# Moving two batches of normalisation statistics on VectorE to other steps of a scan pipeline

## Chip, cores and metric

The kernel runs on one NeuronCore of a Trainium2 chip. The metric is device time in microseconds (us) of one execution, 494.55 us for the kernel before. Five engines work side by side, each through its own queue in order: TensorE (PE in the profile), VectorE (DVE), ScalarE (ACT), GpSimd (POOL) and SyncE (SP), which here only issues DMAs. They meet by semaphores.

## The reference, cut to what matters

Two rows of 2048 tokens with 128 features go through an adaptive layer norm, a Mamba block (a selective scan with 256 inner channels and 16 states), a second adaptive layer norm and a soft decision tree of depth 8.

```python
h = _layernorm(x, axis=-1) * (1 + ca) + sa              # the first norm
xz = h @ W_in;  xp, z = jnp.split(xz, 2, axis=-1)
u = silu(causal_depthwise_conv(xp));  dt_r, Bm, Cm = split(u @ W_xp, ...)
delta = softplus(dt_r @ W_dt + dt_bias)
h_t = exp(delta * A) * h_(t-1) + delta * u * B_t;  y_t = sum_n(h_t * C_t)   # 16 states n, 256 channels
x = x + ga * ((y + u * D_skip) * silu(z)) @ W_out
h = _layernorm(x, axis=-1) * (1 + cb) + sb              # the second norm
gate = sigmoid((h @ Wq.T) @ routers.T);  leaf_prob = product of branch probabilities along each path
x = x + gb * (leaf_prob @ leaf_values @ Wout_w.T + Wout_b)
```

(The lines are shortened; `_layernorm` subtracts the mean over the 128 features and divides by the root of the variance plus 1e-5.)

## The kernel before

The 4096 tokens are cut into 8 groups of 512 (g = 0 to 7, four for each row of the batch). The scan of a group is 32 steps: step s handles state n = s // 2 and half s % 2 of the 256 channels, as a tile of 128 channels by 512 tokens. A main loop over g and s is written out for each engine, and what an engine does is decided by step numbers in tables. In step s of group g:

- ScalarE makes the decay `dA` = exp(delta * a) for the step two ahead (L697, `AHEAD_EXP` = 2) into one of three PSUM banks (`RD` = 3). It may write the bank of step s + 2 once the scan of step s - 1 is done.
- VectorE runs the scan `h` (L1382) with `dA` and `dbu`, and in even steps, for 11 of the 16 states, makes the product `dbu` (L1395) from a PSUM bank `bb` that TensorE has filled (L1148) with B.
- GpSimd makes `dbu` for the other five states (L593) and, when both halves of a state are scanned, the product `hc` = h * C (L606).
- TensorE adds `hc` up in `yb` (L1123), five steps behind the scan.

Beside the scan of group g each engine does its share of the front of group g + 1 (norm, convolution, silu, delta) and of the tail of group g - 1 (second norm, tree) and g - 2. Two of ScalarE's steps hold long blocks, because they change its function table and change it back: step 10 (`F_SILU`: a table load, silu of u and of z, a table load, L764 to L769) and step 17 (`F_SP`: a table load, the softplus of the next delta, from group 2 on also two softplus of the tree, a table load, L794 to L803). In step 10 the exp of scan 12 is issued ahead of the block and that of scan 13 behind it; in step 17 the exp of scan 19 ahead and that of scan 20 behind.

The norms' statistics are made by VectorE in `stats()`: four `bn_stats` (L1254) and four `bn_aggr` (L1257), on tiles of 128 tokens by 128 features. They stand at the end of a step, behind the scan and behind the `dbu` product of that step:

```python
if 4 <= g + 4 < GROUPS and s == N_STATS:          # first norm, of the group four ahead: in g = 0 to 3
    stats(g + 4, f_bn, f_mv[:, g + 4, :, :], s_fvar)
if tail and s == T_STATS:                         # second norm, of group g - 1: in g = 1 to 7
    wait_read(dve, "t", "out", 0, t)
    stats(t, t_bn, t_mv, s_tvar)
```

From the second norm's statistics ScalarE makes 1/sqrt in three small operations (`rstd`, L628 to L630, at `T_RSTD`; the third writes `t_nm`), GpSimd one small product (`t_offset`, L513, at `T_OFF`, ahead of the step's large products), and ScalarE normalises (`t_xhat`, L635, at `T_XHAT` = 24). GpSimd's queue waits at L513 until ScalarE's `rstd` is through. In the last group (g = 7) `rstd`, offset and normalisation stand at steps of their own, `LAST_RSTD`, `LAST_OFF` = 16 and `LAST_XHAT` = 17. The statistics of the first norm are used two groups later than they are made.

Of the kernel before, what the change touches and what calls it, by code (L numbers as in the profile page):

```python
# [7 lines left out]
def bass_adaln_mamba_tree_ffn_kernel(  # L8
# [72 lines left out]

    N_STATS, N_RSTD, N_OFF, N_XHAT = 19, 2, 3, 6
    F_SILU, F_SP, F_DU = 10, 17, (25, 26)
    F_HI, F_R1, F_MID, F_R2, F_LO = 21, 22, 23, 24, 25
    T_GATE, T_STATS, T_RSTD, T_OFF, T_XHAT = (4, 5), 14, 19, 20, 24
    NORMS = {2: (4, 3)}
    NORMS.update({g: (g + 1, g) for g in range(4, GROUPS)})

# [16 lines left out]
    FIRST, LAST = -1, GROUPS - 1  # L107
# [3 lines left out]
              ("node", 1, -1, (23,)), ("lp", 0, -1, (27,)), ("lp", 1, -1, (29,)), ("ff", 0, -1, (STEPS,)))  # L111
    LAST_SP = {2: -2, 25: -1}
    TOKENS = (slice(0, T // 2), slice(T // 2, T))
    LAST_RSTD, LAST_OFF, LAST_XHAT = 16, 16, 17

    def jobs_of(side, g):

# [24 lines left out]
    with ctx:  # L142
# [213 lines left out]
        def wait_job(eng, side, name, part, g):  # L356

            eng.wait_ge(s_job[side], job_at[side, name, part, g] + 1)

        def wait_read(eng, side, name, part, g):  # L360

            eng.wait_ge(s_read[side], read_at[side][job_at[side, name, part, g]])
# [13 lines left out]
        def saves(pair):  # L376

            g, n = divmod(pair, N)
            return (g // CHUNKS) * (CHUNKS - 1) * N + (g % CHUNKS) * N + (n if saved(pair) else 0)

        def saved(pair):

            return pair // N % CHUNKS < CHUNKS - 1

        def by_pool(pair):

            return pair // N * NB + sum(n < pair % N for n in POOL_N)

        def by_dve(pair):

            return pair - by_pool(pair)
# [846 lines left out]
        def _(dve):  # L1238
# [11 lines left out]
            def stats(g, bn, mv, ready):  # L1250
                if g:
                    dve.wait_ge(ready, g)
                for i in range(TILES):
                    last = v.bn_stats(bn[:, i, :], xs[:, g * TILES + i, :])  # L1254
                chain(last)
                for i in range(TILES):
                    last = v.bn_aggr(mv[:, i, :], bn[:, i, :])  # L1257
                last.then_inc(ready, 1)
# [100 lines left out]
            for g in range(FIRST, LAST + 1):  # L1359
                m2, f, t, u = g + 2, g + 1, g - 1, g - 2  # L1360
                norm, tail, leaf = 2 <= m2 < GROUPS, 0 <= t < GROUPS, 0 <= u < GROUPS
                for s in range(STEPS):
                    k = g * STEPS + s
                    if 0 <= k < K:
                        n, half = divmod(s, HALVES)
                        pair = k // HALVES
                        dve.wait_ge(s_dA, k + 1)
                        if half == 0:
                            if n in POOL_N:
                                dve.wait_ge(s_pdbu, by_pool(pair) + 1)  # L1370
                            else:
                                dve.wait_ge(s_dbu, by_dve(pair) + 1)
                            if pair >= RH:

                                dve.wait_ge(s_hc, pair - RH + 1)
                                if saved(pair - RH):
                                    dve.wait_ge(s_save, saves(pair - RH) + 1)
                            if g % CHUNKS:

                                dve.wait_ge(s_save, saves(pair - N) + 1)  # L1380
                        start = state[:, n, half:half + 1] if g % CHUNKS else 0.0
                        v.tensor_tensor_scan(h[:, pair % RH, half, :], dA[k % RD][:, :], dbu[:, pair % RW, half, :],  # L1382
                                             start, ALU.mult, ALU.add).then_inc(s_scan, 1)
                    kd = k + AHEAD_DBU
                    if 0 <= kd < K and kd % HALVES == 0 and kd // HALVES % N not in POOL_N:
                        pair = kd // HALVES
                        gd, n = divmod(pair, N)
                        if n == 0:
                            dve.wait_ge(s_du, HALVES * (gd + 1))
                        mine = by_dve(pair)  # L1390
                        dve.wait_ge(s_fill, mine + 1)
                        if pair >= RW:

                            dve.wait_ge(s_scan, HALVES * (pair - RW + 1))
                        v.tensor_tensor(dbu[:, pair % RW, :, :], du[:, gd % 2, :, :],  # L1395
                                        bb[mine % RB][:, :].unsqueeze(1).broadcast_to([P, HALVES, T]),
                                        ALU.mult).then_inc(s_dbu, 1)
                    if 4 <= g + 4 < GROUPS and s == N_STATS:
                        if g == 0:
                            dve.wait_ge(s_x, 16 * (GROUPS - 4))  # L1400
                        stats(g + 4, f_bn, f_mv[:, g + 4, :, :], s_fvar)
                    if tail and s in T_GATE:

                        half = T_GATE.index(s)
                        hg = HALVES * t + half
                        dve.wait_ge(s_sum, t * STEPS + STEPS - HALVES + half + 1)
                        dve.wait_ge(s_zsilu, t + 1)
                        if t:
                            wait_job(dve, "t", "yt", half, t - 1)
                        else:  # L1410
                            dve.wait_ge(s_wturn, 2)
                        v.tensor_tensor(yg[:, half, :], yb[hg % RY][:, :], zu[:, t % 2, half, :],
                                        ALU.mult).then_inc(s_gate, 1)
                    if tail and s == T_STATS:

                        wait_read(dve, "t", "out", 0, t)
                        stats(t, t_bn, t_mv, s_tvar)
# [69 lines left out]
```

## Time and profile before

| | before |
|---|---|
| median of 3 runs | 494.55 us (493.66 to 495.66) |
| the profiled execution, its own time | 495.33 us |
| its span in the trace | 493.5 us |
| mean granted TensorE clock | 0.941 of full speed |
| VectorE, ScalarE, GpSimd, TensorE busy | 91%, 77%, 86%, 82% |

The span is what the trace covers; the 1.8 us between it and the execution's own time lie around it. All positions below are us from the span's start. A row of a timeline gives start, length from the first start to the last end, engine, source line and operation, output<-inputs with sizes, and how many instructions were merged (x2); in square brackets stands how long the engine sat idle ahead of it and which instruction ended that wait.

### The profile page before, as it was taken

What the parts mean: (1) busy time and instruction counts of PE and PEld (TensorE: products, weight loads), DVE (VectorE), ACT (ScalarE), POOL (GpSimd) and SP (SyncE); (2) the same over time, 40 slices, a digit from 0 to 9 for tenths busy, and PEclk for the clock granted to TensorE, in tenths of its full rate; (3) what the DMA queues carried; (4) which work ended last, traced back from release to release, by engine and by line L of the source; (5) the groups of instructions that cost most, each with busy time, mean ns of one, the idle gap of its engine ahead of it and who ended that gap; (6) DMA issues with size and microseconds to landing.
All of it is one profiled execution on the core that took longest, in us unless ns stands there. A gap on an engine that the chain in (4) does not pass through costs nothing. (4 is left out here: it accounts for less than half of the span.)

```text
span 493.5 us, 6708 instructions
## 1 busy us (share of the span) xinstructions
PE 406.7 (82%) x2133; PEld 279.7 (57%) x2164; DVE 447.3 (91%) x539; ACT 378.1 (77%) x690; POOL 422.7 (86%) x236
## 2 busy tenths in 40 slices
PE   7969665997499698997799788996899697687796
PEld 3537444675358456674558556664658455565474
DVE  6698899979999899989999889988999889999852
ACT  4478975598867898698967898698966898687715
POOL 6159899999999789998999899988999789999810
PEclk9999987997889989998999999998999989599799
DMA  6673045200830028300742027300741027300001
GB/s 168 160 298 151 1 144 222 87 0 1 301 126 27 0 42 327 108 0 2 248 149 77 2 66 303 106 2 0 259 156 60 1 62 306 107 2 21 0 1 43
DMA packets 24146, 51.06 MB, mean 103 GB/s; under 512 B 4521, under 2 KB 14256, under 8 KB 20016
## 3 DMA queue, kind: packets, MB, share of 16 engines
q1 hardware_dynamic: 24112, 50.64, 30.1%
q8 instruction: 17, 0.28, 0.2%
q14 instruction: 17, 0.14, 0.1%
HBM read 48.01 MB, written 2.62 MB: 103 GB/s over the span
## 5 line engine op out<-in xcount | busy, mean ns | idle before, releaser
L606 POOL TENSOR_TENSOR hc<-h,c_rows 128x1024 f32<-128x1024 f32 x127 | 298.4, 2366 | 27.0 <-DVE h L1382 26.3
L1382 DVE TENSOR_TENSOR_SCAN h<-dA,state,dbu 128x512 f32<-128x512 f32 x192 | 234.2, 1266 | 13.2 <-ACT dA L697 13.2
L697 ACT ACTIVATE dA<-delta,a_neg 128x512 f32<-128x512 f32 x256 | 173.2, 685 | 45.3 <-DVE h L1382 44.9
L1123 PE MATMUL yb<-ident,hc 128*128 128x128 f32 x1024 | 155.1, 287 | 17.8 <-POOL hc L606 16.6
L1123 PEld LDWEIGHTS yb<-ident,hc 128*128 128x128 f32 x1024 | 131.0, 149 | 64.9 <-issue 45.0
L1395 DVE TENSOR_TENSOR dbu<-du,bb 128x1024 f32<-128x1024 f32 x88 | 105.5, 1199 | 3.7 <-PE bb L1148 2.0
L593 POOL TENSOR_TENSOR dbu<-du,b_rows 128x1024 f32<-128x1024 f32 x40 | 94.6, 2364 | 4.1 <-DMA b_rows<-bc_dram 4.1
L1382 DVE TENSOR_TENSOR_SCAN h<-dA,dbu 128x512 f32<-128x512 f32 x64 | 74.2, 1205 | 5.5 <-ACT dA L697 5.4
L1023 PE MATMUL mf<-f_hT,w_conv 128*128 128x512 f32 x112 | 54.6, 612 | 2.0 <-ACT zu L757 1.4
L1148 PE MATMUL bb<-b_parts,sel 128*128 128x512 bf16 x63 | 25.1, 399 | 37.7 <-DVE dbu L1395 36.4
L1148 PEld LDWEIGHTS bb<-b_parts,sel 128*128 128x128 bf16 x88 | 8.6, 98 | 56.5 <-DVE dbu L1395 36.9
L1023 PEld LDWEIGHTS mf<-f_hT,w_conv 128*128 128x128 f32 x112 | 19.7, 195 | 17.8 <-issue 14.5
L749 ACT ACTIVATE zu<-mf,cbias 128x512 f32<-128x512 f32 x14 | 9.5, 682 | 18.2 <-PE mf L1023 18.2
L999 PE MATMUL mt<-node_s,path 128*128 128x512 f32 x28 | 16.5, 674 | 7.4 <-ACT probT L833 5.0
L1040 PE MATMUL mf<-zu,w_xp 128*128 128x512 f32 x28 | 21.1, 846 | 1.0 <-ACT delta L794 1.0
L1034 PE MATMUL mf<-w_in,f_hT 128*128 128x128 f32 x128 | 17.7, 281 | 3.4 <-ACT zu L757 3.2
L1113 PEld LDWEIGHTS yb<-diag_d,zu 128*128 128x128 f32 x128 | 17.7, 208 | 3.2 <-issue 2.3
L1113 PE MATMUL yb<-diag_d,zu 128*128 128x128 f32 x128 | 18.9, 295 | 0.0
L703 ACT ACTIVATE state<-h 128x2 f32<-128x2 f32 x96 | 18.5, 193 | 0.2
L1034 PEld LDWEIGHTS mf<-w_in,f_hT 128*128 128x128 f32 x128 | 15.6, 191 | 5.2 <-ACT zu L757 5.2
L1074 PE MATMUL mt<-t_hT,w_node 128*128 128x512 f32 x28 | 15.9, 651 | 2.5 <-ACT node_x L840 2.0
L1048 PE MATMUL mt<-zu,w_xdt 128*128 128x512 f32 x28 | 15.0, 618 | 3.1 <-ACT xs L819 1.6
(206 smaller groups left out, 524.2 us busy)
## 6 DMA issues: line engine op xcount, KB each, us to landing
c_rows<-bc_dram SPq DMA_DIRECT2D x32, 1024.0 KB, 7.5
b_rows<-bc_dram SPq DMA_DIRECT2D x40, 256.0 KB, 8.9
xs<-in_L_attn_x_dram SPq DMA_DIRECT2D x8, 256.0 KB, 3.6
out_dram<-xs SPq DMA_DIRECT2D x7, 256.0 KB, 5.6
ygT<-in_L_attn_conv_w_dram SPq DMA_DIRECT2D x2, 256.0 KB, 4.3
bc_dram<-xd SPq DMA_DIRECT2D x8, 64.0 KB, 1.6
w_in<-in_L_attn_W_in_dram SPq DMA_DIRECT2D x2, 128.0 KB, 4.2
probT<-in_L_wmod_dram SPq DMA_DIRECT2D x1, 256.0 KB, 4.2
```

The costliest lines, as they stand in the source:

```text
L593: nc.gpsimd.tensor_tensor(dbu[:, pair % RW, :, :], du[:, gd % 2, :, :], b_rows[:, i, :].unsqueeze(1).broadcast_to([P, HALVES, T]), ALU.mul ...
L606: nc.gpsimd.tensor_tensor(hc[:, pair % RC, :, :], h[:, pair % RH, :, :], c_rows[:, q, n % NQ, :].unsqueeze(1).broadcast_to([P, HALVES, T]) ...
L697: nc.scalar.activation(dA[ke % RD][:, :], delta[:, ge % 2, half, :], ACT.Exp, scale=a_neg[:, half, n:n + 1]).then_inc(s_dA, 1)
L703: nc.scalar.activation(state[:, pair % N, :], h[:, pair % RH, :, T - 1], ACT.Copy).then_inc(s_save, 1)
L1023: last = nc.tensor.matmul(bank[:, :], w_conv[:, tap, part * P:(part + 1) * P], f_hT[:, tap:tap + T], start=tap == 0, stop=tap == TAPS - 1)
L1034: last = nc.tensor.matmul(bank[:, i * P:(i + 1) * P], f_hT[:, HALO + i * P:HALO + (i + 1) * P], w_in[:, DI + part * P:DI + (part + 1) * P] ...
L1040: last = nc.tensor.matmul(bank[:, :], w_xp[:, piece, :], zu[:, g % 2, HALVES + piece, :], start=piece == 0, stop=piece == HALVES - 1)
L1113: nc.tensor.matmul(bank[:, tile], zu[:, gs % 2, HALVES + half, tile], diag_d[:, half, :], start=tile.start == 0, stop=False, skip_group_ch ...
L1123: last = nc.tensor.matmul(bank[:, tile], hc[:, pair % RC, half, tile], ident[:, :], start=False, stop=n == N - 1, is_transpose=True, skip_ ...
L1148: nc.tensor.matmul(bb[mine % RB][:, :], sel[:, n, :], b_parts[:, gf % 2, :], start=True, stop=True).then_inc(s_fill, 1)
L1382: v.tensor_tensor_scan(h[:, pair % RH, half, :], dA[k % RD][:, :], dbu[:, pair % RW, half, :], start, ALU.mult, ALU.add).then_inc(s_scan, 1)
L1395: v.tensor_tensor(dbu[:, pair % RW, :, :], du[:, gd % 2, :, :], bb[mine % RB][:, :].unsqueeze(1).broadcast_to([P, HALVES, T]), ALU.mult).t ...
```

## The change

The first norm's statistics go from step 19 to step 12, the second norm's from step 14 to step 19, except in the last group, where they stay at 14 under the new name `LAST_STATS`. `rstd` of the second norm goes from step 19 to 21 on ScalarE and its offset from 20 to 22 on GpSimd; `T_XHAT` stays.

```diff
-    N_STATS, N_RSTD, N_OFF, N_XHAT = 19, 2, 3, 6
+    N_STATS, N_RSTD, N_OFF, N_XHAT = 12, 2, 3, 6
     F_SILU, F_SP, F_DU = 10, 17, (25, 26)
-    T_GATE, T_STATS, T_RSTD, T_OFF, T_XHAT = (4, 5), 14, 19, 20, 24
+    T_GATE, T_STATS, T_RSTD, T_OFF, T_XHAT = (4, 5), 19, 21, 22, 24
...
-    LAST_RSTD, LAST_OFF, LAST_XHAT = 16, 16, 17
+    LAST_STATS, LAST_RSTD, LAST_OFF, LAST_XHAT = 14, 16, 16, 17
...
-                    if tail and s == T_STATS:
+                    if tail and s == (LAST_STATS if g == LAST else T_STATS):
```

On VectorE, group 2, from the `dbu` product of step 12 to the scans behind step 19, the rows of before (the operation SCALAR_TENSOR_TENSOR on `h` is the scan):

```order
L1395 TENSOR_TENSOR dbu<-du,bb 128x1024
L1382 SCALAR_TENSOR_TENSOR h<-dA,state,dbu 128x512 x2
L1254 BN_STATS t_bn<-xs 128x6 x4
L1257 BN_AGGR t_mv<-t_bn 128x2 x4
L1382 SCALAR_TENSOR_TENSOR h<-dA,state,dbu 128x512 x2
L1395 TENSOR_TENSOR dbu<-du,bb 128x1024
L1382 SCALAR_TENSOR_TENSOR h<-dA,state,dbu 128x512 x2
L1395 TENSOR_TENSOR dbu<-du,bb 128x1024
L1382 SCALAR_TENSOR_TENSOR h<-dA,state,dbu 128x512
L1254 BN_STATS f_bn<-xs 128x6 x4
L1257 BN_AGGR f_mv<-f_bn 128x2 x4
L1382 SCALAR_TENSOR_TENSOR h<-dA,state,dbu 128x512 x3
```

and the same stretch of VectorE in the changed kernel:

```order
L1395 TENSOR_TENSOR dbu<-du,bb 128x1024
L1254 BN_STATS f_bn<-xs 128x6 x4
L1257 BN_AGGR f_mv<-f_bn 128x2 x4
L1382 SCALAR_TENSOR_TENSOR h<-dA,state,dbu 128x512 x4
L1395 TENSOR_TENSOR dbu<-du,bb 128x1024
L1382 SCALAR_TENSOR_TENSOR h<-dA,state,dbu 128x512 x2
L1395 TENSOR_TENSOR dbu<-du,bb 128x1024
L1382 SCALAR_TENSOR_TENSOR h<-dA,state,dbu 128x512
L1254 BN_STATS t_bn<-xs 128x6 x4
L1257 BN_AGGR t_mv<-t_bn 128x2 x4
L1382 SCALAR_TENSOR_TENSOR h<-dA,state,dbu 128x512 x3
```

The first norm's statistics now stand between the product of step 12 and scan 13, the second norm's between scans 19 and 20, and nothing stands between scans 14 and 15 any more. In groups 4 to 6 there are no statistics of the first norm, so only the second norm's move, from behind scan 14 to behind scan 19.

On ScalarE, group 5, from the exp of scan 21 (issued in step 19) to step 21, before:

```order
L697 ACTIVATE dA<-delta,a_neg 128x512
L628 ACTIVATE t_rs<-t_mv,eps_col 128x4
L629 ACTIVATE t_rs<-t_rs 128x4
L630 ACTIVATE t_nm<-t_rs 128x4
L697 ACTIVATE dA<-delta,a_neg 128x512
L703 ACTIVATE state<-h 128x2
L776 ACTIVATE xd<-mf 128x512
L833 ACTIVATE probT<-mt 128x512
L697 ACTIVATE dA<-delta,a_neg 128x512
L780 ACTIVATE b_parts<-mf 128x512
```

and in the changed kernel:

```order
L697 ACTIVATE dA<-delta,a_neg 128x512 x2
L703 ACTIVATE state<-h 128x2
L776 ACTIVATE xd<-mf 128x512
L833 ACTIVATE probT<-mt 128x512
L697 ACTIVATE dA<-delta,a_neg 128x512
L780 ACTIVATE b_parts<-mf 128x512
L628 ACTIVATE t_rs<-t_mv,eps_col 128x4
L629 ACTIVATE t_rs<-t_rs 128x4
L630 ACTIVATE t_nm<-t_rs 128x4
```

The three `rstd` operations now stand behind the exps of scans 22 and 23 and ahead of that of scan 24.

On GpSimd, one piece of the difference, in each of groups 1 to 6, around the `hc` products of steps 15 to 23:

```order
 L593 TENSOR_TENSOR dbu<-du,b_rows 128x1024
-L606 TENSOR_TENSOR hc<-h,c_rows 128x1024 x2
+L606 TENSOR_TENSOR hc<-h,c_rows 128x1024 x3
 L513 TENSOR_TENSOR t_nm<-t_mv,t_nm 128x4
-L606 TENSOR_TENSOR hc<-h,c_rows 128x1024
 L593 TENSOR_TENSOR dbu<-du,b_rows 128x1024
```

The small product `t_nm` moved behind the `hc` product of scans 20 and 21. TensorE's and SyncE's orders are the same in both kernels.

## Rows read from the trace of the kernel before

**Rows 1.** Busy time on the page: us, share of the span, instructions.

```profile
PE 406.7 (82%) x2133; PEld 279.7 (57%) x2164; DVE 447.3 (91%) x539; ACT 378.1 (77%) x690; POOL 422.7 (86%) x236
```

**Rows 2.** VectorE's waits: us in total, times, longest.

```profile
DVE h L1382 <- ACT dA L697: 18.6, 15, 1.9
```

**Rows 3.** Timeline of group 4, VectorE, scans 13 to 22.

```profile
274.77 2.34 DVE L1382 TENSOR_TENSOR_SCAN h<-dA,dbu 128x512 f32<-128x512 f32 x2 [1.53 <-ACT dA L697]
277.02 0.85 DVE L1254 BATCH_NORM_STATS2 t_bn<-xs 128x6 f32<-128x128 f32 x4
...
278.20 2.31 DVE L1382 TENSOR_TENSOR_SCAN h<-dA,dbu 128x512 f32<-128x512 f32 x2
...
287.74 3.45 DVE L1382 TENSOR_TENSOR_SCAN h<-dA,dbu 128x512 f32<-128x512 f32 x3 [1.62 <-ACT dA L697]
```

**Rows 4.** The same group on ScalarE: exps of scans 18 and 19, softplus block.

```profile
279.43 0.69 ACT L697 ACTIVATE dA<-delta,a_neg 128x512 f32<-128x512 f32 x1 [1.58 <-DVE h L1382]
...
280.54 0.69 ACT L697 ACTIVATE dA<-delta,a_neg 128x512 f32<-128x512 f32 x1 [0.30 <-DVE h L1382]
281.25 1.28 ACT L794 ACT_TABLE_LOAD   x1
```

**Rows 5.** Timeline of groups 0 and 1, VectorE.

```profile
53.74 4.57 DVE L1382 TENSOR_TENSOR_SCAN h<-dA,dbu 128x512 f32<-128x512 f32 x4 [1.85 <-ACT dA L697]
...
65.01 3.42 DVE L1382 TENSOR_TENSOR_SCAN h<-dA,dbu 128x512 f32<-128x512 f32 x3
...
90.53 1.22 DVE L1395 TENSOR_TENSOR dbu<-du,bb 128x1024 f32<-128x1024 f32 x1 [0.54 <-PE bb L1148]
...
108.47 2.46 DVE L1382 TENSOR_TENSOR_SCAN h<-dA,state,dbu 128x512 f32<-128x512 f32 x2 [1.53 <-ACT dA L697]
...
121.33 3.60 DVE L1382 TENSOR_TENSOR_SCAN h<-dA,state,dbu 128x512 f32<-128x512 f32 x3
```

**Rows 6.** Timeline of group 3, VectorE: scan 13 and scan 20.

```profile
219.52 2.46 DVE L1382 TENSOR_TENSOR_SCAN h<-dA,state,dbu 128x512 f32<-128x512 f32 x2 [1.40 <-ACT dA L697]
...
232.73 3.63 DVE L1382 TENSOR_TENSOR_SCAN h<-dA,state,dbu 128x512 f32<-128x512 f32 x3 [0.27 <-ACT dA L697]
```

**Rows 7.** Windows, groups 1 and 2: PE, PEld, DVE, ACT, POOL busy; PEclk, DMA share, GB/s.

```profile
82.90:138.40 55.50, 45.27 (x228) 31.65 (x231) 52.38 (x61) 41.91 (x80) 53.85 (x31) 0.84 0.28 101
138.40:193.90 55.50, 48.56 (x266) 33.56 (x268) 53.47 (x62) 47.17 (x93) 50.96 (x25) 0.97 0.27 90
```

**Rows 8.** Timeline of groups 0 and 1, GpSimd: all its waits from 50 to 135 us.

```profile
55.04 4.69 POOL L606 TENSOR_TENSOR hc<-h,c_rows 128x1024 f32<-128x1024 f32 x2 [1.70 <-DVE h L1382]
...
113.35 2.35 POOL L606 TENSOR_TENSOR hc<-h,c_rows 128x1024 f32<-128x1024 f32 x1 [0.43 <-DVE h L1382]
...
123.83 2.35 POOL L606 TENSOR_TENSOR hc<-h,c_rows 128x1024 f32<-128x1024 f32 x1 [1.01 <-DVE h L1382]
```

**Rows 9.** Timeline, TensorE, where group 1 begins.

```profile
82.43 1.97 PE L1123 MATMUL yb<-ident,hc 128*128 128x128 f32 x8 [2.54 <-POOL hc L606]
84.19 3.50 PE L1023 MATMUL mf<-f_hT,w_conv 128*128 128x512 f32 x4
...
87.96 1.88 PE L1023 MATMUL mf<-f_hT,w_conv 128*128 128x512 f32 x4
```

**Rows 10.** Timeline of group 5, all engines, behind the softplus block.

```profile
343.18 3.63 DVE L1382 TENSOR_TENSOR_SCAN h<-dA,state,dbu 128x512 f32<-128x512 f32 x3 [1.45 <-ACT dA L697]
...
343.80 0.28 ACT L628 ACTIVATE t_rs<-t_mv,eps_col 128x4 f32<-128x4 f32 x1
...
344.46 0.67 ACT L697 ACTIVATE dA<-delta,a_neg 128x512 f32<-128x512 f32 x1
...
345.72 2.36 POOL L606 TENSOR_TENSOR hc<-h,c_rows 128x1024 f32<-128x1024 f32 x1 [0.89 <-DVE h L1382]
...
347.21 0.69 ACT L697 ACTIVATE dA<-delta,a_neg 128x512 f32<-128x512 f32 x1
...
347.85 2.45 DVE L1382 TENSOR_TENSOR_SCAN h<-dA,state,dbu 128x512 f32<-128x512 f32 x2
```

## The prediction

> **What bounds the kernel now.** I read the page's busy shares first: VectorE is busy 447.3 of 493.5 us, GpSimd 422.7, ScalarE 378.1 [rows 1]. So VectorE is the engine to watch, with GpSimd close behind it. Then VectorE's waits: the largest item is its scan waiting for a decay tile from ScalarE, 18.6 us in 15 waits, at most 1.9 us each [rows 2]. Then the timeline of one group, to see where these lie. In group 4 VectorE has two stalls. One of 1.53 us ends at 274.77, at scan 13, behind ScalarE's silu block; the other of 1.62 us ends at 287.74, at scan 20, behind the softplus block [rows 3]. Between them stand the second norm's statistics: they begin at 277.02 and the next scan begins at 278.20, so the eight small instructions push the scans back by 278.20 - 277.02 = 1.18 us [rows 3]. That is the price of one batch of statistics, and the reader should see that VectorE pays it at full price 1.5 us after having stood idle for longer than that.
>
> The other groups: in groups 0 and 1 the stall at scan 13 is 1.85 and 1.53 us [rows 5], in group 3 it is 1.40 [rows 6]. At scan 20 the row carries no wait in groups 0 and 1 [rows 5], a wait of 0.27 us in group 3 [rows 6], 1.62 in group 4 [rows 3] and 1.45 in group 5 [rows 10]. In groups 0 to 3 the first norm's statistics stand right ahead of scan 20, which is why little or nothing is left of the stall there. Group 2 looks like group 3, group 6 like group 5.
>
> **The change, part by part.** *Groups 4, 5 and 6.* The second norm's batch leaves the full-price place behind scan 14 and goes ahead of scan 20, where VectorE idles 1.62 and 1.45 us. Both are above 1.18, so it costs nothing there; some 0.44 and 0.27 us of stall should remain. The gain is 1.18 us a group, if the end of the softplus block moves forward by the same amount. It does so if the block's start hangs on VectorE and not on a ScalarE that is behind. ScalarE's rows say so: the exp of scan 18 waited 1.58 us for a scan, that of scan 19 another 0.30 us, and the block begins right behind it at 281.25 [rows 4]. Take 1.18 us away from VectorE, and the first of these waits shrinks to 0.40; ScalarE is still the one that waits, so the block starts 1.18 us earlier. Three groups give 3.54 us.
>
> *Groups 1, 2 and 3.* Two batches change place. The first norm's goes from ahead of scan 20 to ahead of scan 13, under a stall of 1.53, 1.5 and 1.40 us, hence for nothing (cover left over: 0.2 to 0.35 us). The second norm's takes the place it left, at the same price there, whatever that is: nothing in groups 2 and 3, the full 1.18 in group 1. What vanishes is the batch behind scan 14, again 1.18 us a group, 3.54 us in all. ScalarE's exp 13 hangs on its own silu block, which starts before the batch, so nothing is delayed by it.
>
> *Group 0* has only a first norm's batch, moved from ahead of scan 20, where no stall covers it [rows 5], to scan 13, under 1.85 us. VectorE saves 1.18 us locally. But GpSimd, released by scan 13 at 55.04 (a time that does not move), has no wait at all until 113.35 [rows 8]: 58 us at full load, because this stretch also holds the scaling of the output weights. TensorE waits 2.54 us for one of these `hc` products at 82.43, and then TensorE is busy until VectorE, at 90.53, waits 0.54 us for its `bb` bank [rows 5, 9]. So VectorE arrives earlier and waits 1.72 instead of 0.54. I count 0 for group 0; the bounds are 0 and 1.18.
>
> *Group 7* keeps its place: 0.
>
> *`rstd` from step 19 to 21.* It takes 344.46 - 343.80 = 0.66 us of ScalarE [rows 10] and moves from ahead of exp 22 to ahead of exp 24. Exp 24 ran at 347.21 to 347.90; what stood ahead of it is the same in sum, so its end should stay there to 0.1 us, and scan 24 begins half of the row's 2.45 us behind 347.85, at about 349.07 [rows 10]. The cover is 1.2 us. If it were gone, each us late would cost VectorE one us. *`t_offset` from step 20 to 22.* GpSimd waits there for `rstd`, with the `dbu` product of state 14 and the next `hc` queued behind it. `rstd` should be through at about 347.3, GpSimd comes out of its `hc` product at 345.72 + 2.36 = 348.08 [rows 10], so it does not wait: 0. If it did, it would be by less than it idles before scan 15 (0.43 us in group 1 [rows 8]). The normalisation in step 24 lies behind both.
>
> The sum: 6 x 1.18 = 7.1 us. On the profiled execution's own time, 495.33 - 7.1 = 488.2. That execution lies 0.8 us above the median of the three runs, 494.55; taken from the median, **487.5 us**.
>
> **Is there room on GpSimd?** In group 1, the tightest, it is busy 53.85 of 55.5 us, in group 2 50.96 [rows 7]. A group shorter by 1.18 us leaves 0.5 and 3.4 us. In group 1 itself, GpSimd waits 0.43 us at 113.35 and 1.01 us at 123.83, both for a scan [rows 8]. With the batch gone, the scan that releases it at 123.83 comes at 122.65; GpSimd, which can start 0.43 earlier and no longer has `t_nm` in between, is ready at about 122.2. It waits still, so group 1 keeps its 1.18. The waits in that group add up to 1.44, just above 1.18: this is the thinnest margin of the sum. The Trainium skill (Perfetto Trace Analysis, "GPSIMD Engine Instruction") warns that a GpSimd instruction's reported span is unreliable and that start-to-start spacing should be used. Here two products take 4.69 us from the first start to the last end, against 2 x 2.35 of single ones [rows 8], so by either reading the sum above stands.
>
> **The rivals.**
> 1. *Group 0 keeps its gain too.* For it: VectorE has no stall from 65.01 to 90.53 in the rows. Against it: the 0.54 us wait at 90.53, which leads through TensorE to a GpSimd at full load. 495.33 - 7 x 1.18 = 487.1, against the median 486.3.
> 2. *GpSimd takes the gain back in the early groups.* If GpSimd is what groups 1 to 3 really run at, their three gains turn into VectorE waits for `bb` or `hc`, and 3.5 us are left: 491.0. Rows 7 speak for it in group 1 (97% busy) and against it in groups 2 and 3 (92%).
> 3. *No change.* The stalls move instead of filling: the softplus block's start hangs on ScalarE, and scan 20 waits 1.2 us longer in every group. For it speaks that ScalarE has just come out of the silu block; against it the waits of 1.58 and 0.30 us. 494.5.
> 4. *Slower: TensorE's clock.* In group 1 the granted clock is 0.84, in group 2 0.97 [rows 7]; at 84.19, behind the wait of 2.54 us, four convolution products took 3.50 us against 1.88 at 87.96 [rows 9], the lower and the higher of the two levels, 1.2 and 2.4 GHz. If a shifted rhythm put two such batches of four at the lower level in each of groups 2 to 6, TensorE would be late by 2 x 1.62 us five times, 16.2 us, less the gain of 7.1: 503.6. It decides from 7.1 / 5 = 1.4 us a group, nearly one batch. The Trainium skill (TensorE: Matmul & The Clock Gate, "What's actually happening") has the gate halve the clock when the array was idle lately. By that rule this rival needs longer idle times of TensorE than before. The change makes the group shorter and leaves TensorE its work, so its idle time falls; that speaks against.
>
> **How the numbers follow.** My forecast has 0.64, rival 1 0.08, rival 2 and its like (one to four of the six gains lost) 0.15, rival 3 0.09, rival 4 0.04. A measurement of this kernel tells about 0.5%, 2.5 us, from no change; at least three gains of six pass that. Faster by over 0.5%: 0.64 + 0.08 + 0.14 = 0.86. Within 0.5%: 0.09 + 0.01 = 0.10. Slower: 0.04. The range goes down to rival 1 with 0.7 us for the spread of the runs, 485.6, and up to rival 2, 491.0.
>
> **What would show it.** In the changed trace: in groups 1 to 6 the row from scan 14 to scan 17 has no statistics in it; the wait ahead of scan 13 is 0.15 to 0.7 us in groups 0 to 3 and still about 1.5 in 4 to 6; the wait ahead of scan 20 is 0.3 to 0.45 in groups 4 to 6; the total of VectorE's waits for `dA` falls from 18.6 us by about 4 x 1.2 + 3 x 1.2 = 8.3 to some 10 us; ScalarE's wait ahead of exp 18 falls from 1.58 to about 0.4; the wait for `bb` at the start of group 1 grows to about 1.7. The prediction is wrong if that last growth is seen in later groups too, if ScalarE has no wait left ahead of the softplus block, if GpSimd waits for `rstd` at L513, or if the granted clock of groups 2 to 6 drops below 0.97.

## The result, and the profile after

The changed kernel takes 486.33 us (median of 6 runs, 485.41 to 488.33), beside 494.3 us for the kernel before in the same set. The ratio is 0.984, with a 95% interval of 0.9817 to 0.9863: 8 us faster, with 7.1 forecast. The page of the changed kernel (the profiled execution took 488.33 us) begins with these two rows, span and busy shares, beside [rows 1]:

```profile
span 486.5 us, 6739 instructions
...
PE 404.0 (83%) x2164; PEld 274.6 (56%) x2164; DVE 447.5 (92%) x539; ACT 377.1 (77%) x690; POOL 422.0 (87%) x236
```

VectorE does the same 447.5 us of work; the span is shorter because it stands idle less. The waits of VectorE, beside [rows 2]:

```profile
DVE h L1382 <- ACT dA L697: 9.9, 14, 1.5
...
DVE dbu L1395 <- PE bb L1148: 5.8, 7, 1.4
```

The wait for the decay tile fell from 18.6 to 9.9 us, a little more than the 8.3 worked out ahead. The second row was 2.0 us before the change; 4.0 of its 5.8 us lie ahead of 52 us, at a place that the change does not touch, and come back with the experiments. Group 4 on VectorE, the rows that answer to [rows 3]:

```profile
273.61 4.57 DVE L1382 TENSOR_TENSOR_SCAN h<-dA,dbu 128x512 f32<-128x512 f32 x4 [1.53 <-ACT dA L697]
...
283.70 0.84 DVE L1254 BATCH_NORM_STATS2 t_bn<-xs 128x6 f32<-128x128 f32 x4
284.58 0.38 DVE L1257 BATCH_NORM_AGGREGATE t_mv<-t_bn 128x2 f32<-128x6 f32 x4
285.40 3.45 DVE L1382 TENSOR_TENSOR_SCAN h<-dA,dbu 128x512 f32<-128x512 f32 x3 [0.45 <-ACT dA L697]
```

and on ScalarE, the rows that answer to [rows 4]:

```profile
277.09 0.69 ACT L697 ACTIVATE dA<-delta,a_neg 128x512 f32<-128x512 f32 x1 [0.40 <-DVE h L1382]
...
278.21 0.69 ACT L697 ACTIVATE dA<-delta,a_neg 128x512 f32<-128x512 f32 x1 [0.30 <-DVE h L1382]
278.92 1.28 ACT L794 ACT_TABLE_LOAD   x1
```

Scans 13 to 16 now run without a gap (x4). The statistics stand where 1.62 us of stall were, and 0.45 are left. From scan 13 to scan 20 it is 285.40 - 273.61 = 11.79 us, before it was 287.74 - 274.77 = 12.97: 1.18 saved. ScalarE's wait ahead of the exp of scan 18 went from 1.58 to 0.40, as forecast to the hundredth.

The following table is not a view but worked out from the timelines: the start of scan 13 in each group, in us, and the start of scan 28 of group 7. From scan 13 of group 1 to that point lies everything that the change can reach except group 0.

| | before | before, 2nd trace | after | first only | second only |
|---|---|---|---|---|---|
| group 0, scan 13 | 53.74 | 55.21 | 56.72 | 55.39 | 54.97 |
| group 1, scan 13 | 108.47 | 109.04 | 110.52 | 109.25 | 108.80 |
| group 4, scan 13 | 274.77 | 275.06 | 273.61 | 274.37 | 274.71 |
| group 7, scan 28 | 465.44 | 465.73 | 460.38 | 465.04 | 461.45 |
| groups 1 to 7, difference | 356.97 | 356.69 | 349.86 | 355.79 | 352.65 |
| from scan 28 to the end | 28.1 | 26.2 | 26.1 | 26.7 | 26.2 |

The stretch shortened by 356.97 - 349.86 = 7.11 us; forecast were 6 x 1.18 = 7.08. The starts of scan 20 of group 0 and of scan 28 that are used below stand inside merged rows; they were read from narrow windows, good to 0.03 us.

### The profile page after: what moved, and what is told of

Its sections match the earlier page's. It is cut to its first block and busy times, and to the rows that moved or that the text cites. A ratio compares the mean times of both kernels' runs of the same rounds, so it can differ in the third digit from the quotient of the medians.

```text
span 486.5 us, 6739 instructions
## 1 busy us (share of the span) xinstructions
PE 404.0 (83%) x2164; PEld 274.6 (56%) x2164; DVE 447.5 (92%) x539; ACT 377.1 (77%) x690; POOL 422.0 (87%) x236
## 5 line engine op out<-in xcount | busy, mean ns | idle before, releaser
L1123 PEld LDWEIGHTS yb<-ident,hc 128*128 128x128 f32 x1024 | 127.8, 146 | 65.5 <-issue 40.8
L1123 PE MATMUL yb<-ident,hc 128*128 128x128 f32 x1024 | 151.4, 282 | 12.6 <-POOL hc L606 12.6
L1148 PE MATMUL bb<-b_parts,sel 128*128 128x512 bf16 x88 | 35.0, 398 | 34.5 <-DVE dbu L1395 33.2
L1074 PE MATMUL mt<-t_hT,w_node 128*128 128x512 f32 x28 | 17.2, 699 | 2.0 <-ACT node_x L840 1.5
L612 POOL TENSOR_TENSOR du<-delta,zu 128x512 f32<-128x512 f32 x14 | 17.5, 1271 | 0.0
```

Of the source, the lines that this page charges most:

```text
L612: nc.gpsimd.tensor_tensor(du[:, f % 2, half, :], delta[:, f % 2, half, :], zu[:, f % 2, HALVES + half, :], ALU.mult).then_inc(s_du, 1)
L1123: last = nc.tensor.matmul(bank[:, tile], hc[:, pair % RC, half, tile], ident[:, :], start=False, stop=n == N - 1, is_transpose=True, skip_ ...
L1148: nc.tensor.matmul(bb[mine % RB][:, :], sel[:, n, :], b_parts[:, gf % 2, :], start=True, stop=True).then_inc(s_fill, 1)
```

## The experiments

In each of the four sets of experiments the kernel before ran as well; a ratio is always to those runs, and where a sentence says "faster" or "slower" in us without naming medians, it is the ratio times about 494 us. The intervals are 0.7 to 1.2 us wide to either side. The changed kernel itself was repeated once, as yardstick of the first set.

**The changed kernel again.** No edit.

> The changed kernel once more, as the yardstick of this set: 0.984 of the kernel before, some 8 us shorter. The other kernels of the set are read against it and against the kernel before.

Measured: 486.76 us, ratio 0.9853 (0.9834 to 0.9872), 7.3 us faster. The gain holds.

**Only the first norm's statistics moved.**

```diff
-    T_GATE, T_STATS, T_RSTD, T_OFF, T_XHAT = (4, 5), 19, 21, 22, 24
+    T_GATE, T_STATS, T_RSTD, T_OFF, T_XHAT = (4, 5), 14, 19, 20, 24
```

> Only the first norm's statistics move (19 to 12); the second norm's stay at 14, with rstd at 19 and the offset at 20. Cover theory (a batch of 1.18 us is free where ScalarE's block keeps VectorE waiting, and is paid elsewhere): groups 2 and 3 gain nothing, since the batch was covered at 19 already and the stall ahead of scan 20 comes back at about 1.5 us; groups 4 to 6 are unchanged; group 1 saves 1.18, group 0 between 0 and 1.18. In all 1.2 to 2.4 us below the kernel before, 492 to 493. Rival theory (each place is worth the same by itself, the order around scan 13 matters more than the cover): 4 x 1.18 = 4.7 us below before.

Measured: 492.87 us, ratio 0.9968 (0.9952 to 0.9983), 1.6 us faster (the medians are 2.0 apart). In the table, the stretch of groups 1 to 7 is 1.18 us shorter than before: group 1 alone. In group 2 VectorE's timeline shows why the other groups gain nothing; the stall is back where the first norm's batch was taken away:

```profile
174.14 1.27 DVE L1382 TENSOR_TENSOR_SCAN h<-dA,state,dbu 128x512 f32<-128x512 f32 x1
176.86 3.63 DVE L1382 TENSOR_TENSOR_SCAN h<-dA,state,dbu 128x512 f32<-128x512 f32 x3 [1.45 <-ACT dA L697]
```

**Only the second norm's statistics moved.**

```diff
-    N_STATS, N_RSTD, N_OFF, N_XHAT = 12, 2, 3, 6
+    N_STATS, N_RSTD, N_OFF, N_XHAT = 19, 2, 3, 6
```

> Only the second norm's statistics move (14 to 19, with the scales at 21 and 22); the first norm's stay at 19, so in groups 1 to 3 both batches stand ahead of scan 20. Cover theory: groups 4 to 6 gain 1.18 each; groups 2 and 3 have 2.36 us of statistics under a stall of 1.45, pay 0.9 and save 1.18, so gain 0.3 each; group 1 pays for both as before. In all 3.54 + 0.6 = 4.1 us below before, about 490.2. Rival theory (places are worth the same by themselves): 6 x 1.18 = 7.1 us below before.

Measured: 489.5 us, ratio 0.9911 (0.9893 to 0.9929), 4.4 us faster (the medians are 5.4 apart). The stretch is 4.32 us shorter, expected were 4.1. Two batches in a row in group 2, 2.34 us from the first one's start to the next scan, use up the stall and stick out by the rest:

```profile
174.59 0.84 DVE L1254 BATCH_NORM_STATS2 f_bn<-xs 128x6 f32<-128x128 f32 x4
...
176.93 3.60 DVE L1382 TENSOR_TENSOR_SCAN h<-dA,state,dbu 128x512 f32<-128x512 f32 x3
```

A place is worth what stall is left in it, not a fixed 1.18 us: the rival that each move earns by itself falls (it wanted 4.7 and 7.1 us).

**Group 0's batch back at step 19.**

```diff
-                    if 4 <= g + 4 < GROUPS and s == N_STATS:
+                    if 4 <= g + 4 < GROUPS and s == (N_STATS if g else 19):
```

> As the changed kernel, but group 0 makes the first norm's statistics at step 19 as before; groups 1 to 3 at 12. If GpSimd at full load takes group 0's gain (my theory), the time is that of the changed kernel to 0.3 us. If group 0 keeps its gain (rival 1), it is 1.18 us longer than the changed kernel.

Measured: 486.83 us, ratio 0.9856 (0.9837 to 0.9876), the yardstick's time. Scan 13 of group 0 began at 56.68 in this trace and 56.72 in the changed kernel's, scan 20 at 67.95 and 66.81, so the batch is paid for in the one and not in the other. Scan 13 of group 1 began at 110.52 in both. Group 0's 1.18 us are lost by then; rival 1 falls. It falls by the traces: the intervals of the two ratios alone would not clearly part 1.18 us from nothing. The kernel before bears it out, for in its second trace scan 13 of group 1 begins 109.04 - 55.21 = 53.83 us behind that of group 0, in the changed kernel 110.52 - 56.72 = 53.80. VectorE's timeline of the changed kernel has two waits in between that show part of the way:

```profile
83.07 1.22 DVE L1395 TENSOR_TENSOR dbu<-du,bb 128x1024 f32<-128x1024 f32 x1 [0.53 <-POOL du L612]
...
104.03 1.22 DVE L1395 TENSOR_TENSOR dbu<-du,bb 128x1024 f32<-128x1024 f32 x1 [0.96 <-PE bb L1148]
```

The first is absent with the batch at step 19, the second is 0.59 there: 0.90 us of the 1.18. The wait that the prediction named, at the start of group 1 behind TensorE, is in neither: the gain went to other places than it said, GpSimd's `du` among them. That GpSimd is at full load throughout is read from the traces: in the changed kernel, the only wait for another engine that it has from 50 to 135 us is the one in this row (the next one ends at 165.99), and not even group 1 has one any more, where [rows 8] had two.

```profile
58.02 4.68 POOL L606 TENSOR_TENSOR hc<-h,c_rows 128x1024 f32<-128x1024 f32 x2 [1.71 <-DVE h L1382]
```

No kernel with less work on GpSimd was run, so the place is shown and the engine only argued.

**The kernel before, a second trace.** No edit.

> The kernel before once more, for its trace alone. Two stretches of its first trace that no changed line touches differ from all traces of changed kernels: the start of group 0 (scan 13 began at 53.74 us, in the others at 54.97 to 56.72) and the end (from scan 28 of group 7 to the end 28.1 us, in the others 26.1 to 26.7). If that is TensorE's clock, which differs between executions, this trace has other values in them. If it belongs to the kernel, it has the same values.

Measured: 493.65 us, span 491.9. Scan 13 of group 0 begins at 55.21 instead of 53.74, and from scan 28 of group 7 to the end it is 26.2 us instead of 28.1. So start and end differ between executions of the same program, by 1.5 and 1.9 us. For the start the windows from 30 to 40 us show part of the reason. First the first trace of the kernel before, then the second, then the changed kernel:

```profile
30.00:40.00 10.00, 8.00 (x28) 3.74 (x27) 9.87 (x9) 7.34 (x18) 8.82 (x5) 1.00 1.00 398
```

```profile
30.00:40.00 10.00, 8.00 (x19) 3.26 (x18) 8.52 (x8) 6.41 (x15) 8.53 (x5) 0.83 1.02 404
```

```profile
30.00:40.00 10.00, 8.12 (x19) 4.02 (x20) 7.66 (x8) 5.61 (x14) 7.34 (x5) 0.66 1.02 413
```

The granted clock, third from the end, is 1.00, 0.83 and 0.66 here. What the clock costs is read from a fixed row ahead of the window to scan 13 of group 0, in the same order:

```profile
29.57 1.16 PE L1034 MATMUL mf<-w_in,f_hT 128*128 128x128 f32 x8 [0.69 <-ACT zu L757]
```

```profile
29.34 1.16 PE L1034 MATMUL mf<-w_in,f_hT 128*128 128x128 f32 x8 [0.69 <-ACT zu L757]
```

```profile
30.09 1.95 PE L1034 MATMUL mf<-w_in,f_hT 128*128 128x128 f32 x8 [0.69 <-ACT zu L757]
```

From there it is 53.74 - 29.57 = 24.17 us, 55.21 - 29.34 = 25.87 and 56.72 - 30.09 = 26.63: 1.7 us for the clock of 0.83 and 2.5 for that of 0.66. The rest of the difference was there at 30 us already; its cause stays open. The kernel with only the second norm moved agrees: its clock is 1.00 there too, it takes 54.97 - 30.80 = 24.17 us, and its scan 13 is late by the start alone. With the lower clock go the changed kernel's larger waits for `bb` ahead of 52 us. The end goes the same way: from 463 to 468 us the granted clock is 0.50 in the first trace of the kernel before and 1.00 in the second, and the four products of TensorE around 464 us take 3.75 and 1.95 us. In the stretch between, the two traces differ by 0.28 us.

**Both batches one step later.**

```diff
-    N_STATS, N_RSTD, N_OFF, N_XHAT = 12, 2, 3, 6
+    N_STATS, N_RSTD, N_OFF, N_XHAT = 13, 2, 3, 6
...
-    T_GATE, T_STATS, T_RSTD, T_OFF, T_XHAT = (4, 5), 19, 21, 22, 24
+    T_GATE, T_STATS, T_RSTD, T_OFF, T_XHAT = (4, 5), 20, 21, 22, 24
```

> The changed kernel with both batches of statistics one step later: the first norm's at 13, behind scan 13, the second norm's at 20, behind scan 20. Cover theory: both stand behind the scan that waits for ScalarE, so no batch is covered. Against the kernel before, group 1 pays for two as before, groups 4 to 6 for one as before, groups 2 and 3 pay 1.18 more each: 2.4 us longer than before, 9.4 us longer than the changed kernel. Rival theory (VectorE's order matters little, what helped is that the scales on ScalarE and GpSimd stand later, which they do here too): as the changed kernel to 1 us.

Measured: 499.01 us, ratio 1.0089 (1.0066 to 1.0113): slower than the kernel before. One step decides between 8 us won and 4.4 lost. Group 5 on VectorE has the stall and, behind the scan that ends it, the batch at full price, 349.56 - 348.39 = 1.17 us:

```profile
347.19 1.28 DVE L1382 TENSOR_TENSOR_SCAN h<-dA,state,dbu 128x512 f32<-128x512 f32 x1 [1.45 <-ACT dA L697]
348.39 0.84 DVE L1254 BATCH_NORM_STATS2 t_bn<-xs 128x6 f32<-128x128 f32 x4
...
349.56 2.43 DVE L1382 TENSOR_TENSOR_SCAN h<-dA,state,dbu 128x512 f32<-128x512 f32 x2
```

From scan 13 of group 1 (111.44) to scan 28 of group 7 (470.74) it is 359.30 us, 2.33 more than before, where 2.4 were expected. The other 2 us lie between scan 13 of group 0 (55.38) and that of group 1: 56.06 us, against 54.73 and 53.83 in the two traces of before. The granted clock from 80 to 90 us goes with it, 0.50 here against 0.66 and 0.83, and VectorE then waits 1.33 us for `bb` at 93.50; further it was not taken apart. That the scales stand late in this kernel too, and that it is slow all the same, speaks against the rival that they brought the gain.

**The scales of the second norm early again.**

```diff
-    T_GATE, T_STATS, T_RSTD, T_OFF, T_XHAT = (4, 5), 19, 21, 22, 24
+    T_GATE, T_STATS, T_RSTD, T_OFF, T_XHAT = (4, 5), 19, 19, 20, 24
```

> The changed kernel with rstd of the second norm back at step 19 and its offset at 20; both batches of statistics where the change has them. Cover theory: the statistics are through before ScalarE comes out of its softplus block, so nothing waits for them and the time is that of the changed kernel to 0.5 us. Rival theory (the later scales bring part of the gain): longer by up to 0.66 us in each of six groups, 4 us.

Measured: 491.14 us, ratio 0.9921 (0.99 to 0.9942): by the ratios 3.4 to 4 us longer than the changed kernel. Here my theory said no difference, and the rival was right in size. The statistics were indeed through in time; the loss appears behind scan 20. Group 5 on TensorE, ScalarE and VectorE in this kernel, behind the softplus block:

```profile
343.32 1.75 PE L999 MATMUL mt<-node_s,path 128*128 128x512 f32 x2 [1.94 <-ACT probT L833]
344.86 1.91 PE L1000 MATMUL mt<-node_x,path 128*128 128x512 f32 x2
...
346.81 0.60 ACT L833 ACTIVATE probT<-mt 128x512 f32<-128x512 f32 x1 [1.74 <-PE mt L1000]
...
347.90 1.22 DVE L1395 TENSOR_TENSOR dbu<-du,bb 128x1024 f32<-128x1024 f32 x1 [0.56 <-PE bb L1148]
```

and the same on TensorE in the changed kernel:

```profile
341.77 1.12 PE L999 MATMUL mt<-node_s,path 128*128 128x512 f32 x2 [1.28 <-ACT probT L833]
342.74 1.02 PE L1000 MATMUL mt<-node_x,path 128*128 128x512 f32 x2
```

`rstd`, 0.66 us long, stands ahead of ScalarE's reading of the first leaf sums (L833). TensorE, which may only then write the second, waits 1.94 us instead of 1.28, and the same four products take 3.45 us instead of 1.99. The windows of this kernel show the granted clock before and in that stretch:

```profile
340.20:343.30 3.10, 1.18 (x10) 0.85 (x8) 3.07 (x3) 3.04 (x10) 1.77 (x3) 1.00 0.00 0
343.30:347.20 3.90, 3.88 (x8) 1.83 (x9) 3.90 (x4) 2.16 (x5) 3.90 (x2) 0.56 0.52 84
```

The clock is at its lower level for most of the second window, 1.2 instead of 2.4 GHz, after 3.1 us in which TensorE was busy for 1.18. ScalarE then waits 1.74 us, and VectorE has a wait of 0.56 us for `bb` and a further one of 0.62 us at scan 28. From scan 20 to scan 28, group 5 takes 13.24 us instead of 11.68, group 2 13.24 instead of 11.67, group 4 11.70 instead of 11.29, the others what they took. In all the stretch of groups 1 to 7 is 352.75 us, 2.9 longer than in the changed kernel; the rest of the 3.4 to 4 us does not show in this trace.

**A product pulled into the stall that is left.** In groups 4 to 6 the product `dbu` of state 9 and its filling move from steps 16 and 15 to step 12 (on TensorE; on VectorE alike):

```diff
+                    if g in PULL_G and s == 12:
+                        kf = g * STEPS + 18
+                    elif g in PULL_G and s == 15:
+                        kf = -1
```

> The changed kernel, and in groups 4 to 6, where 1.53 us of stall ahead of scan 13 are left, the product dbu of state 9 (1.11 us) and TensorE's filling of its bank are pulled from steps 16 and 15 into step 12. The filling can begin only when the product of state 7 has read the bank, so some 0.3 us of the product stick out and 0.8 are gained; ScalarE has 0.40 + 0.30 us of lead left ahead of its softplus block, which bounds the gain at 0.7 a group. Expected: 3 x 0.7 = 2 us below the changed kernel. If ScalarE's lead is the limit sooner, nothing is gained.

Measured: 487.49 us, ratio 0.9856 (0.9838 to 0.9874): nothing gained. Group 4 on VectorE (line numbers are five higher here; L1387 is the scan):

```profile
272.18 1.22 DVE L1406 TENSOR_TENSOR dbu<-du,bb 128x1024 f32<-128x1024 f32 x1 [0.48 <-PE bb L1153]
273.31 6.79 DVE L1387 TENSOR_TENSOR_SCAN h<-dA,dbu 128x512 f32<-128x512 f32 x6
...
285.10 3.45 DVE L1387 TENSOR_TENSOR_SCAN h<-dA,dbu 128x512 f32<-128x512 f32 x3 [1.58 <-ACT dA L698]
```

The stall ahead of scan 13 is filled, and the 1.1 us reappear at scan 20: 1.58 instead of 0.45. From scan 13 to 20 it is 11.79 us as in the changed kernel. The product of step 16 stands behind scan 16, and scan 16 is the one that releases the exp of scan 19 and with it the softplus block. Taking away work behind it moves no block. My expectation had overlooked on which side of that scan the product stood.

**Both batches as early as that scan allows, and one step earlier.**

```diff
-    N_STATS, N_RSTD, N_OFF, N_XHAT = 12, 2, 3, 6
+    N_STATS, N_RSTD, N_OFF, N_XHAT = 9, 2, 3, 6
...
-    T_GATE, T_STATS, T_RSTD, T_OFF, T_XHAT = (4, 5), 19, 21, 22, 24
+    T_GATE, T_STATS, T_RSTD, T_OFF, T_XHAT = (4, 5), 16, 21, 22, 24
```

> The changed kernel with the first norm's statistics at step 9 instead of 12 and the second norm's at 16 instead of 19. The pulled product of the last set brought nothing: it stood behind scan 16, and it is scan 16 that releases the exp of scan 19 and with it the softplus block. So the anchor theory now says that everything on VectorE between the scan that releases the block (9 for silu, 16 for softplus) and the scan behind the stall (13 and 20) shares the stall's cover, wherever it stands: as the changed kernel to 0.5 us. Rival theory (the batch must stand right ahead of the waiting scan): some of it is paid, up to 7 us longer.

Measured: 487.83 us, ratio 0.9858 (0.9835 to 0.9881), the changed kernel's ratio within the intervals. The second kernel has `T_STATS` = 15 and `N_STATS` = 12:

> The changed kernel with the second norm's statistics at step 15, one step ahead of the other kernel's 16 and so ahead of scan 16. Anchor theory: they hold up scan 16, the exp of scan 19 and the block; groups 2 to 6 pay 1.18 us each, 5.9 us longer than the changed kernel. Rival theory (a batch may stand anywhere between the blocks as long as it is near enough): 1 us or less.

Measured: 493.24 us, ratio 0.9982 (0.9965 to 0.9998): nearly all of the gain is gone, with one step between the two. VectorE in group 4 of the kernel with step 16, from the product ahead of the batch to the stall at scan 20:

```profile
276.82 1.19 DVE L1395 TENSOR_TENSOR dbu<-du,bb 128x1024 f32<-128x1024 f32 x1
277.93 0.86 DVE L1254 BATCH_NORM_STATS2 t_bn<-xs 128x6 f32<-128x128 f32 x4
...
284.13 3.45 DVE L1382 TENSOR_TENSOR_SCAN h<-dA,dbu 128x512 f32<-128x512 f32 x3 [0.46 <-ACT dA L697]
```

and in group 5 of the kernel with step 15, where the row between the batch and the product is scan 16:

```profile
334.07 0.84 DVE L1254 BATCH_NORM_STATS2 t_bn<-xs 128x6 f32<-128x128 f32 x4
...
335.25 1.25 DVE L1382 TENSOR_TENSOR_SCAN h<-dA,state,dbu 128x512 f32<-128x512 f32 x1
...
343.73 3.63 DVE L1382 TENSOR_TENSOR_SCAN h<-dA,state,dbu 128x512 f32<-128x512 f32 x3 [1.45 <-ACT dA L697]
```

Behind scan 16 the batch is covered in full (0.46 left, as with step 19); ahead of it, it is paid for, and the stall stays at 1.45. In the stretch of groups 1 to 7 the second kernel takes 355.54 us, 5.7 more than the changed one; expected were 5.9.

So the edge is shown for the softplus block. For the silu block only one side of it was tried, no kernel has the batch ahead of scan 9, and the result is mixed: with `N_STATS` = 9 the stall at scan 13 shrinks to 0.43 and 0.22 us in groups 2 and 3, but in group 1 it is 1.53 still, and scan 13 of group 1 comes 109.89 - 54.65 = 55.24 us behind that of group 0 instead of 53.80. VectorE waited 1.59 us for `bb` at 91.95 in that stretch, where the changed kernel has no such wait; whether the batch's place or the execution brought it was not taken apart.

**The scales at step 20, and at step 22.**

```diff
-    T_GATE, T_STATS, T_RSTD, T_OFF, T_XHAT = (4, 5), 19, 21, 22, 24
+    T_GATE, T_STATS, T_RSTD, T_OFF, T_XHAT = (4, 5), 19, 20, 21, 24
```

> The changed kernel with rstd at 20 and the offset at 21, one step earlier. In step 20 rstd stands ahead of ScalarE's reading of the first leaf sums (L833), which TensorE waits for before the second (L999); in step 21 behind it. At step 19 it cost about 4 us, and there TensorE's wait grew by the 0.66 us of rstd, its granted clock fell to half in three groups, and ScalarE and VectorE then waited for it. If this is the cause, step 20 costs the same as step 19: 3 to 4 us longer than the changed kernel. Rival theory (it is ScalarE's backlog right behind the softplus block): half of it or less, since the exps of scans 21 and 22 go first.

Measured: 490.94 us, ratio 0.9935 (0.9912 to 0.9958), 4 to 5 us behind the changed kernel, as at step 19; the rival of the backlog falls. The "three groups" of the expectation are not what the trace with step 19 shows: behind the waits it speaks of the clock fell in two groups, 2 and 5. It was also at 0.50 from 228 to 230 and from 392 to 394 us, ahead of scan 20 of groups 3 and 6, and cost nothing there. The other one has 22 and 23:

> The changed kernel with rstd at 22 and the offset at 23, one step later; rstd stands behind the first reading of the leaf sums and ahead of the second. By both theories as the changed kernel to 1 us: the first reading is not delayed, the second by 0.66 us, but its product then is not followed by a wait of TensorE of that length. If it is slower by 2 us or more, any delay of a reading of leaf sums costs.

Measured: 488.06 us, ratio 0.9878 (0.9858 to 0.9897), by the ratios 1.2 to 1.9 us longer than the changed kernel, a little over the 1 us expected and under the 2 us that would have told the other way. The trace, which is of its fastest run, shows nothing of that: its stretch of groups 1 to 7 is 349.85 us, the changed kernel's 349.86. So by the traces what counts is the side of L833 on which `rstd` stands, not how far it is from the block. In the kernel with step 20, TensorE's wait is 1.94 us in group 5 as well, but there the clock held:

```profile
345.14 1.12 PE L999 MATMUL mt<-node_s,path 128*128 128x512 f32 x2 [1.94 <-ACT probT L833]
346.10 1.02 PE L1000 MATMUL mt<-node_x,path 128*128 128x512 f32 x2
```

and VectorE took 11.68 us from scan 20 to 28, as in the changed kernel. It took 13.23 in group 2 and 13.39 in group 4, and there the granted clock stood at half at 180 and at 290 us. The 0.66 us cost nothing by themselves; they cost 1.6 to 2.1 us where the clock falls on them.

No kernel tried is faster than the changed one.

## Why the prediction was right

**The price of a batch, 1.18 us, and the cover in six groups.** Right, and shown from both sides: one step behind the stall the batches cost (1.0089), and in the trace each of groups 1 to 6 is 1.16 to 1.18 us shorter between scans 13 and 20. The later scales brought nothing of it: no kernel moved them alone, but from scan 20 to 28 groups 1, 2, 3, 5 and 6 take 11.6 to 11.7 us before and after. The condition that the prediction set, that ScalarE waits for VectorE ahead of the block, is met with the forecast 0.40 and 0.30 us. What it did not say is the exact edge: cover reaches back to the scan that releases the block (16), not only to the scan ahead of the stall. Two of its figures are off without weight: the batch begins 277.02 - 274.77 = 2.25 us behind the end of the stall, not 1.5, and its 4 x 1.2 + 3 x 1.2 is 8.4 (8.3 is 7 x 1.18).

**Group 0 gives nothing.** Right, by the kernel that takes its move back; but the way there was another one than the wait for `bb` that the prediction named. It forecast that this wait grows from 0.54 to about 1.7 us, and there is none at that place in the changed kernel. The median alone would have misled: 486.33 us is the 486.3 of rival 1, which the traces refute. The 0.9 us beyond the 7.1 lie in the start and the end (see below), so the agreement is chance.

**Room on GpSimd.** Right in what it concluded: scan 20 of group 1 came at 122.21 - 110.52 = 11.69 us behind scan 13 instead of 12.86, the full gain. The working was not: the prediction had GpSimd still waiting in group 1 and took the 1.44 us of its waits as the margin. In the changed kernel it has no wait left there, and in the second trace of the kernel before it has only this one from 60 to 135 us:

```profile
124.40 2.35 POOL L606 TENSOR_TENSOR hc<-h,c_rows 128x1024 f32<-128x1024 f32 x1 [0.58 <-DVE h L1382]
```

So the waits differ between executions, and 0.58 us are less than the 1.18 that were saved all the same. Group 1 kept its gain with no wait of GpSimd left; how late GpSimd may get before it costs was not measured.

**`rstd` and `t_offset` moved, counted at nothing.** The size was right for the kernel as changed: GpSimd's `t_nm` has no wait (the row at 344.20 stands directly behind the product of 341.88), and the exp of scan 24 did not become late.

```profile
341.88 2.37 POOL L606 TENSOR_TENSOR hc<-h,c_rows 128x1024 f32<-128x1024 f32 x1 [1.55 <-DVE h L1382]
344.20 0.21 POOL L513 TENSOR_TENSOR t_nm<-t_mv,t_nm 128x4 f32<-128x4 f32 x1
```

But the reasoning looked only at what stands ahead of exp 24 "in sum". Within that sum the reading of the leaf sums changes side, and with it TensorE's wait. With the statistics moved and the scales left where they were, the change would have brought half: 0.9921. The prediction had no term for that.

**The rival of the clock.** It did not come in the changed kernel, where five windows of some 55 us from 140 us on, about one a group, have a clock of 0.97 to 1.00, but the mechanism is real: it is what made the kernels with early scales slower, with 1.6 to 2.1 us for a drop in the wrong place, near the 1.62 us for four products at the lower level that the prediction used. Part of it shows in the changed kernel too: at the border of groups 3 and 4 the clock falls (246 to 248 us at 0.50), which it does not do in either trace of before but does in the repeat of the changed kernel, and in group 4 VectorE then waits 0.58 us for `bb` in a place where it did not:

```profile
267.12 1.22 DVE L1395 TENSOR_TENSOR dbu<-du,bb 128x1024 f32<-128x1024 f32 x1 [0.58 <-PE bb L1148]
```

The trace with the scales at 22 has both too (a wait of 0.48 us). The one with statistics at 9 and 16 has neither. Against this 0.6 us stands a wait of 0.40 us ahead of scan 28 of group 4, which is gone. The two nearly cancel, which by luck helped the sum to look as exact as it does: 7.11 against 7.08, where two executions of the kernel before already differ by 0.28.

**The last 0.9 us.** The medians differ by 8 us, the stretch that the sum describes by 7.1. The rest lies in the start and the end, where two executions of the same program differ by more than that (the profiled executions, 495.33 and 488.33 us, have a later start for the changed kernel and an end 2 us shorter). Whether the change shifts their average stays open; the repeat of the changed kernel, at 7.3 us by its ratio, leaves 0.2 us to explain.

## What to carry to other kernels

When an engine A waits at regular places for a long block of engine B, find the instruction of A that releases that block. Work of A between that instruction and the stall is free up to the length of the stall; the same work one instruction ahead of it or one behind the stall costs its full length, and work that was already in the free stretch gains nothing by being moved. Here this was shown on both sides for one block, the softplus block in groups 2 to 6. Before small operations on B are moved or left, look at which reading of B a third engine waits for: its order among them can be worth more than its length.

## What the runs showed of the hardware

TensorE's clock reacted to a difference of 0.66 us in a wait, and not each time. Ahead of the second leaf sums of groups 2 to 6, waits of 1.94 to 1.99 us stand eight times in the traces: three times each in the kernels with the scales at 19 and at 20, once in the second trace of the kernel before (group 5) and once with only the first norm's statistics moved (group 6). After four of the eight, all with early scales and moved statistics, the products ran at the lower level (in group 5 at 19, 0.56 of full speed over the next 3.9 us); after the other four they did not, nor after any of the waits of 1.53 us and less at this place. The Trainium skill (TensorE: Matmul & The Clock Gate, "What's actually happening") says that the chip's watch over activity runs freely and does not start with the kernel. By that rule the same wait may or may not be hit. The traces agree: a granted clock of 1.00 and of 0.83 from 30 to 40 us in two executions of the kernel before.
